# A state-space scan: the order of a round redone, one set of zero-weight products in place of two, and one copy from PSUM moved to VectorE

## What is computed

```python
def _ssm(h, in_w, xproj_w, dt_bias, A_log, Dskip, out_w):
    ...
    dt = jax.nn.softplus(proj[..., :D_INNER] + dt_bias)
    Bm = proj[..., D_INNER:D_INNER + D_STATE]
    Cm = proj[..., D_INNER + D_STATE:]
    A = -jnp.exp(A_log)
    def step(hst, ins):
        dt_t, B_t, C_t, x_t = ins
        dA = jnp.exp(dt_t[:, :, None] * A)
        hst = hst * dA + (dt_t * x_t)[:, :, None] * B_t[:, None, :]
        y_t = jnp.einsum('bds,bs->bd', hst, C_t)
        return (hst, y_t)
    _, ys = jax.lax.scan(step, h0, (tm(dt), tm(Bm), tm(Cm), tm(xs)))
    y = jnp.swapaxes(ys, 0, 1) + xs * Dskip
    return y * jax.nn.silu(z) @ out_w
```

## Time and profile before

| | us |
|---|---|
| median of 3 runs | 7119.47 (7112.84 to 7120.07) |
| the profiled execution | 7115.03 |
| its span, first to last instruction | 7113.3 |

### The profile page before, as it was taken

How to read it: one execution, slowest core, us unless ns; L and a number is a source line. 1 busy time by engine, 2 the same in 40 slices (tenths; PEclk the granted TensorE clock), 3 DMA queues, 4 the chain that set the end, 5 groups by cost and what they waited for, 6 DMA issues and landing times. The chain is left out here.

```text
span 7113.3 us, 205317 instructions
## 1 busy us (share of the span) xinstructions
PE 6393.6 (90%) x85792; PEld 3192.1 (45%) x85792; DVE 4188.9 (59%) x6974; ACT 4613.4 (65%) x9618; POOL 3331.1 (47%) x2816
## 2 busy tenths in 40 slices
PE   6888679999999999999999999979899999978988
PEld 3444434444444444444444444434355445444544
DVE  2555556666666666666666666655344445445554
ACT  3555478888888888888888888852244345345554
POOL 0011156666666666666666666640033223224432
PEclk8999879999999999999999999989999999989999
DMA  6555522222222222222222222235200000010000
GB/s 192 150 142 138 159 68 59 59 58 58 65 60 58 59 58 65 60 59 58 59 59 66 59 59 59 58 123 201 95 7 7 10 7 10 4 35 13 10 13 7
DMA packets 596363, 459.87 MB, mean 65 GB/s; under 512 B 449728, under 2 KB 504640, under 8 KB 577280
## 3 DMA queue, kind: packets, MB, share of 16 engines
q1 hardware_dynamic: 594408, 444.73, 21.5%
q10 hardware_dynamic: 1048, 2.16, 0.1%
HBM read 301.29 MB, written 145.49 MB: 63 GB/s over the span
## 5 line engine op out<-in xcount | busy, mean ns | idle before, releaser
L1472 POOL TENSOR_TENSOR s_dec<-s_hs,s_dec 128x512 f32<-128x512 f32 x2040 | 2561.5, 1281 | 1212.7 <-DVE s_hs L1512 791.9
L1393 ACT ACTIVATE s_dec<-s_pa 128x512 f32<-128x512 f32 x4096 | 2268.9, 618 | 403.8 <-PE s_pa L1246 403.6
L1501 DVE TENSOR_TENSOR s_pA<-s_pA,s_dec 128x512 f32<-128x512 f32 x2040 | 1393.0, 694 | 830.3 <-ACT s_hs L1399 563.9
L1512 DVE TENSOR_TENSOR s_hs<-s_pB,s_dec 128x512 f32<-128x512 f32 x2040 | 1330.9, 684 | 338.1 <-PE s_py L1283 236.8
L1283 PE MATMUL s_py<-s_hs,s_cz 128*32 128x256 f32 x16384 | 1392.4, 418 | 0.0
L1399 ACT COPY s_hs<-s_pA 128x512 f32<-128x512 f32 x2048 | 1210.3, 599 | 205.0 <-PE s_pA L1256 201.8
L1292 PE MATMUL s_py<-s_still 128*32 128x512 bf16 x15848 | 1243.2, 386 | 0.0
L1246 PE MATMUL s_pa<-s_dl,s_al 18*128 18x64 bf16 x32768 | 958.9, 192 | 79.7 <-DMA s_dl<-D 48.6
L1256 PE MATMUL s_pA<-az 18*128 18x256 bf16 x4096 | 778.7, 285 | 180.5 <-DVE s_pA L1501 176.5
L1256 PE MATMUL s_pB<-az 18*128 18x256 bf16 x4096 | 826.5, 283 | 3.5 <-DMA az<-U 3.5
L2067 POOL TENSOR_TENSOR t_prob<-t_prob,t_rinv 128x512 f32<-128x512 f32 x512 | 528.7, 1039 | 508.5 <-DVE t_rinv L2440 508.5
(11 more groups left out here) (260 smaller groups left out, 6395.2 us busy)
## 6 DMA issues: line engine op xcount, KB each, us to landing
s_dl<-D SPq DMA_DIRECT2D x512, 144.0 KB
az<-U SPq DMA_DIRECT2D x1024, 72.0 KB
az<-B SPq DMA_DIRECT2D x1024, 36.0 KB
D<-p_dp SPq DMA_DIRECT2D x64, 384.0 KB, 5.8
U<-p_up SPq DMA_DIRECT2D x60, 384.0 KB, 6.3
B<-p_bz SPq DMA_DIRECT2D x144, 128.0 KB, 2.5
SZ<-p_sz SPq DMA_DIRECT2D x16, 1024.0 KB, 4.0
SK<-p_skip SPq DMA_DIRECT2D x16, 1024.0 KB, 5.8
```

What stands on the lines that cost most here:

```text
L1393: act.activation(dec[w][:].rearrange("p k i t d -> p (k i t) d")[:, :, DS * q + d:DS * q + d + 8], pa[:, bank, :].rearrange("p (d c) -> p ...
L1472: pool.tensor_tensor(m, two(hs[k][:, (x + 1) % 2, :]), m, ALU.mult).then_inc(m_done, 1)
L1501: dve.tensor_tensor(state, state, of_chunk(k, x), ALU.mult).then_inc(mul, 1)
L1512: dve.tensor_tensor(out, two(pB[:, k - 2, :]), of_chunk(k, x), ALU.add).then_inc(added, 1)
```

## The change

- `keep_warm` makes one set instead of two, always onto `py`; the two calls onto `pB` in round 1 are gone.
- `adt` calls the hook before its third and fifth step instead of before its first and fourth.
- TensorE's order in a quiet round: A0; y of the round before last, half 1; a set; B3 of this round; w0 with A1 beside; y of the last round, half 0; a set; w1 with B2 of the next round beside. Rounds 0 and 8 begin with that y, the set, B3, w0, y half 0, a set and only then A0; then w1, A1, y half 1, B2. Rounds 1 and 9 have their own order.
- VectorE's order: multiply 0, addition 3 of the last round, multiply 1, addition 2. In rounds 0 and 8 the addition comes ahead of the wait for the decays. The addition of chunk 3 has thus moved from its own round into the next.
- `copied` becomes `copied0` and `copied1`. In rounds 7 and 15 VectorE makes the copy of chunk 1 (`copy_1`), ScalarE elsewhere.
- ScalarE's copy of chunk 0 also waits for `y_mm`, half 1 of the y of two rounds before.

```diff
                 def adt(p, w, banks, beside=None):
-                    if beside:
-                        beside(0)
                     wait(pe, taken, 2 * p - 1)
                     for i in range(8):
-                        if beside and i == 3:
-                            beside(1)
+                        if beside and i in (2, 4):
+                            beside(i // 2 - 1)
...
-                def keep_warm(onto):
-
-                    for _ in range(2):
+                def keep_warm():
+
+                    for _ in range(1):
                         for k in range(CH):
-                            pe.matmul(onto[QR * k:QR * (k + 1), :], still[:, W:W + QR], still[:, 0:W],
+                            pe.matmul(py[QR * k:QR * (k + 1), :], still[:, W:W + QR], still[:, 0:W],
...
+                        if x % TB == 0:
+                            if n:
+                                y(n - 2, (x - 2) % BODY, 1)
+                                keep_warm()
+                            to_b3()
+                            make(0, None)
+                            if n:
+                                y(n - 1, old, 0)
+                                keep_warm()
+                            to_a(n, x, 0, 0)
+                            to_a(n, x, 0, 1)
+                            make(1, None)
+                            to_a1(0)
+                            to_a1(1)
+                            if n:
+                                y(n - 1, old, 1)
                             to_b2(0)
                             to_b2(1)
...
+                        elif x % TB == 1:
+                            to_a(n, x, 0, 0)
+                            to_a(n, x, 0, 1)
+                            make(0, None)
+                            to_b3()
+                            if x == 9:
+                                keep_warm()
+                            to_a1(0)
+                            to_a1(1)
+                            if x == 1:
+                                make(1, None)
+                                wait(pe, ytok_done, G)
+                                wait(pe, c_filled, 2 * G + 1)
+                                y(n - 1, old, 0)
+                                keep_warm()
+                                to_b2(0)
+                                to_b2(1)
+                            else:
+                                wait(pe, c_filled, 2 * G + 2)
+                                y(n - 1, old, 0)
+                                keep_warm()
+                                make(1, to_b2)
+                        else:
+                            to_a(n, x, 0, 0)
+                            to_a(n, x, 0, 1)
+                            y(n - 2, (x - 2) % BODY, 1)
+                            keep_warm()
+                            to_b3()
+                            make(0, to_a1)
+                            y(n - 1, old, 0)
+                            keep_warm()
+                            make(1, to_b2 if ahead else None)
...
                 def copy_a(n, x, k):
+                    if k == 0:
+                        wait(act, y_mm, 2 * n - 2)
                     wait(act, bu_a, 2 * n + k + 1)
...
-                            copy_a(n, x, 1)
+                            if x % TB != TB - 1:
+                                copy_a(n, x, 1)
...
+                def copy_1(n, x):
+                    wait(dve, bu_a, 2 * n + 2)
+                    dve.tensor_copy(hs[1][:, x % 2, :], pA[:, 1, :]).then_inc(copied1, 1)
...
+                        if x % TB == 0 and n:
+                            plus(n - 1, 3)
                         dec_ready(dve, G, x, head)
-                        for k in range(2):
-                            times(n, x, k, start)
+                        times(n, x, 0, start)
+                        if x % TB:
+                            plus(n - 1, 3)
+                        times(n, x, 1, start)
                         if x == 1 and not head:
                             take_y(G)
-                        for k in range(2, CH):
-                            plus(n, made, x, k, start)
+                        plus(n, 2)
+                        if x % TB == TB - 1:
+                            copy_1(n, x)
```

More of the change, by code:

```diff
@@ L1113, in scan @@
         a_in = [sem(f"a_in{e}") for e in range(4)]
-        (c_in, y_out, zeroed, const, mul, bu_a, copied, bu_b, added, m_done, y_mm, filled, taken, c_filled,
+        (c_in, y_out, zeroed, const, mul, bu_a, copied0, copied1, bu_b, added, m_done, y_mm, filled, taken, c_filled,
          ytok_done, exp_ready) = (
-            sem(n) for n in ("c_in", "y_out", "zeroed", "const", "mul", "bu_a", "copied", "bu_b", "added", "m_done",
+            sem(n) for n in ("c_in", "y_out", "zeroed", "const", "mul", "bu_a", "copied0", "copied1", "bu_b", "added", "m_done",
                              "y_mm", "filled", "taken", "c_filled", "ytok_done", "exp_ready"))
@@ L1278, in y @@
                     if v == 0:
-                        wait(pe, copied, 2 * n + 2)
+                        wait(pe, copied0, n + 1)
+                        wait(pe, copied1, n + 1)
                         wait(pe, added, 2 * n + 2)
@@ L1317, in body, with to_a1 @@
                         more = not (last and x >= TB)
-                        late = x == 1
-                        before = (x - 1) % BODY
-                        has = not (head and x == 0)
                         ahead = not (last and x == BODY - 1)
-                        def to_a0(v):
-                            to_a(n, x, 0, v)
+                        old = (x - 1) % BODY
+                        def to_a1(v):
+                            to_a(n, x, 1, v)
                         def to_b2(v):
-                            if late and v == 0:
-                                wait(pe, added, 2 * n + 1)
-                                keep_warm(pB[:, 0, :])
@@ L1330, in to_b2 @@
                             to_b(n + 1, (x + 1) % BODY, G + (x + 1) // BODY, 2, v)
[L1332 to L1352, removed]
+                        def to_b3():
+                            if n:
+                                for v in range(2):
+                                    to_b(n, x, G, 3, v)
@@ new lines, in make @@
+                        def make(w, beside):
+                            if more:
+                                produce(G, x, w, head, turn, beside)
+                            elif beside:
+                                beside(0)
+                                beside(1)
+                        if x % TB == 0:
[12 more added lines that the diff above has]
+                            to_a1(1)
+                            if n:
+                                y(n - 1, old, 1)
@@ L1382, in _ @@
                 bodies(body)
+                y(BODY * ALL - 2, BODY - 2, 1)
                 y(BODY * ALL - 1, BODY - 1, 0)
@@ L1397, in copy_a @@
                 def copy_a(n, x, k):
+                    if k == 0:
+                        wait(act, y_mm, 2 * n - 2)
                     wait(act, bu_a, 2 * n + k + 1)
-                    act.copy(hs[k][:, x % 2, :], pA[:, k, :]).then_inc(copied, 1)
+                    act.copy(hs[k][:, x % 2, :], pA[:, k, :]).then_inc(copied1 if k else copied0, 1)
                 def take_pair(G, x, w, head):
@@ L1495, in times @@
                 def times(n, x, k, first):
-                    wait(dve, copied, 2 * n + k - 1)
+                    wait(dve, copied1 if k else copied0, n)
                     if first:
@@ L1501, in times, with plus @@
                         dve.tensor_tensor(state, state, of_chunk(k, x), ALU.mult).then_inc(mul, 1)
-                def plus(n, made, x, k, first):
+                def plus(n, k):
+                    G, x = n // BODY, n % BODY
+                    made = 2 * (n - G // BODIES)
                     wait(dve, bu_b, 2 * n + k - 1)
@@ L1507, in plus @@
                     out = two(hs[k][:, x % 2, :])
-                    if first:
+                    if n % (BODY * BODIES) == 0:
                         dve.tensor_copy(out, two(pB[:, k - 2, :])).then_inc(added, 1)
                     else:
-                        wait(dve, m_done, made + 2 * x + k - 3)
+                        wait(dve, m_done, made + k - 3)
                         dve.tensor_tensor(out, two(pB[:, k - 2, :]), of_chunk(k, x), ALU.add).then_inc(added, 1)
+                def copy_1(n, x):
+                    wait(dve, bu_a, 2 * n + 2)
+                    dve.tensor_copy(hs[1][:, x % 2, :], pA[:, 1, :]).then_inc(copied1, 1)
                 def take_y(G):
@@ L1523, in body @@
                         start = first and x == 0
+                        if x % TB == 0 and n:
+                            plus(n - 1, 3)
                         dec_ready(dve, G, x, head)
-                        for k in range(2):
-                            times(n, x, k, start)
+                        times(n, x, 0, start)
```

(9 more changed lines are left out.)

## The result

The changed kernel takes 6945.94 us, median of 4 runs (6929.75 to 7066.31), against 7117.27 us before; the ratio is 0.9754, with a 95% interval of 0.974 to 0.9767. Forecast were 6575 us and a range of 6460 to 6810: the direction was right, a third of the saving came.

A forecast was written before the change was run, and what follows sets the result against it. TensorE bounds quiet rounds by a hair (3.02 us), and seams cost 2.8 us each. A body of 50.5 us plus 0.7 for clock falls, times 64, gives a 3275 us scan, saving 538 from 7115: 6575 us, range 6460 to 6810.

The forecast's parts named there:

- The seam of round 8: Between blocks of 8 rounds: a seam costs 1.1 us instead of 2.8, round 8's exponentials no longer waiting for VectorE.
- The quiet round: In the scan: 2.92 us instead of 3.02, with ScalarE's 2.90 now longer than TensorE's 2.82.
- The body at full clock: Sixteen rounds of the scan: 16 x 2.92 + 1.1 + 1.27 + 1.4 = 50.5 us, before 59.6.
- The copy on VectorE: Rounds 7 and 15: 0.24 us won a seam, its 0.68 us costing nothing in 2.13 us of idle time.
- rival D: Seams: VectorE's copy locks out GpSimd on the path, up to 6660 us; chance 0.05.
- The loads: U and B loads in the scan: costed at nothing; 26 us if four runs a body came 0.1 us late each.
- The clock: In the scan: most bodies keep 2.4 GHz; one body in six falls, 4 us lost each, 0.7 a body.
- rival A: The clock falls in every body of the scan as before, 64 x 54.5 = 3488, 6790 us; chance 0.22.
- rival B: In the scan the clock does not come back up, rounds run at 4.9 us, at most 8560 us; chance 0.05.

The follow-up runs named there:

- gap_fill_half: The gap-filling kernel without the zero-weight set behind the first y of quiet rounds; 7043.93 us (6866.12 to 7124.9).
- gap-filling kernel: The changed kernel with seven more zero-weight sets a body where TensorE waits, in rounds 0, 1, 2, 8 and 9; 6601.78 us, again 6594.27 us.
- gap_fill_first: The changed kernel with only the four added zero-weight sets of rounds 0, 1 and 2; 6822.17 us, ratio 0.96 to before.
- two_sets: The changed kernel with two sets of zero-weight products a call instead of one; 7225.59 us, ratio 1.0156 to before.

## Why the prediction was wrong

1. The seam of round 8, right. The walk gives 8 x 2.92 + 1.1 = 24.5 us for the block of round 8, measured 24.32. Round 8 took 2.06 us as walked through, VectorE's idle time 1.24.
2. The quiet round, right: 2.94 against 2.92, with ScalarE unbroken; gap_fill_half, whose TensorE has a set less to do, has 2.94 too.
3. The body at full clock, right: 50.5 forecast, 50.91 and 50.64 in the two gap-filling kernels shown. The changed kernel itself has no body that is wholly at full clock.
4. The copy on VectorE, right in size: 0.24 us a seam walked, 0.18 measured at full clock and 0.26 in the whole time. But the prediction says that it runs beside GpSimd's product of chunk 3, and that is not so. GpSimd's last product before the seam shown ends at 2163.41 and the copy starts at 2163.45; in 127 of the 128 seams the two do not overlap. So this copy could not test rival D. VectorE's other PSUM copy, of `py`, could, as in the new order it does fall beside GpSimd's products:

```profile
2160.73 2.68 POOL L1494 TENSOR_TENSOR s_dec<-s_hs,s_dec 128x512 f32<-128x512 f32 x2 [1.36 <-DVE s_hs L1536]
...
2132.07 4.98 POOL L1494 TENSOR_TENSOR s_dec<-s_hs,s_dec 128x512 f32<-128x512 f32 x4 [2.59 <-ACT s_dec L1412]
2136.01 0.68 DVE L1546 COPY wa<-s_py 128x512 f32<-128x512 f32 x1
```

In 63 of 64 bodies it overlaps a product; both keep their durations, 0.68 and 1.28 us, and four products in a row take 4.98 us with the copy beside them, after 4.97 in the kernel before. D shows nowhere.

5. The loads: no term was needed. TensorE waits for U once in the scan, 1.7 us.
6. The clock, wrong, and it is nearly the whole miss. The step reads "most bodies should keep 2.4 GHz. ... I take one body in six", at 4 us lost a fall. At 64 x 50.91 = 3258 us the scan would have been 408 us shorter than its 3666, and 7115 - (3813 - 3258) = 6560 us. Instead some 1170 us went by at 1.2 GHz, each costing 0.35 us. The sum had 64 x 0.7 = 45 us for this. What was mis-sized is above all the number of falls: 90 and not 11. Their price was nearly right, 408 / 90 = 4.5 us and not 4, for a mean length of 12.6 us and not 10.2; the 20.48 us of the body shown is not typical. "One in six" had no row behind it. I compared the longest idle times with those of before and looked for the emptiest stretch of rounds 8 and 9 alone, and not at rounds 1 and 2, where all but one of the bodies fall, although rival A names the waits of round 1. And I set the thinned seam of round 8 beside one of before that had six zero-weight sets between its start and A1 of round 9, where the new order has two. The length depends on the sets: 7 to 10 us with two sets a call; with one, mostly 14 to 27 or just 3.4; up to 498 with one of its two calls gone.
7. Rival A named the right mechanism at too low a price: 4 us a body, where it was 408 / 64 = 6.4, as there was twice the time at 1.2 GHz in a body, 18 us after 8, part of it at the second seam. Part of rival B, held for 5 in 100, is there too: a quiet round at 1.2 GHz took 4.8 us, as it said, and in 27 of the 64 bodies more than half of the first block ran so. But the clock came back each time, after 48 us at most for stretches that begin in the scan, and the whole was faster, not slower.

Why the new order starts a second fall in rounds 9 and 10, even with two sets a call, no run separates: the places of A, B and y changed together.

The Trainium skill, TensorE: Matmul & The Clock Gate, Part 1, says that activity releases the throttle. Two kernels that differ in where seven sets stand (and in two waits), 6602 and 7003 us, agree with it as far as falling goes, and I had weighed it too lightly. For coming back it is not enough as it stands: gap_fill_half was busy for 415.93 of 418.00 us and stayed at 0.50.

## What to carry to other kernels

Work that only keeps TensorE's clock up has two uses here, and they sit in different places. Where the engine waits it prevents a fall, at almost no cost. In the busy rounds it prevents few falls (three begin in the scan with it, seven without), but without it they last longer: one set fewer in a quiet round cost 450 us by the medians. So thin such work by place and not by rate, and try each place by itself. After a change that shortens TensorE's work, price each round at both clock levels and ask separately what would start a fall and what TensorE is doing when the clock should come back. And judge an order by its rounds at full clock: with its idle places filled the changed kernel takes 0.93 of the time before, and without 0.975. How much of the 0.93 the new order alone is worth is not shown, since no run fills the idle places of the old order, which spent 540 us at 1.2 GHz itself.

## What the runs showed of the hardware

- At 1.2 GHz a TensorE that is busy without a printed gap (20.40 of 20.40 us in gap_fill_first, 415.93 of 418.00 in gap_fill_half) is not thereby given its clock back; with two zero-weight sets a call (before, two_sets) it came back after 7 to 10 us in nearly every body.
- The clock can fall without a long idle time. Just ahead of 85 of the changed kernel's 90 falls TensorE has no printed idle time over 0.35 us; before, the usual fall came behind one of 1.13.
- A float32 copy from PSUM on VectorE (0.68 us) and a float32 product of GpSimd (1.28 us) ran side by side 63 times without either taking longer.
- A body can be in step with the clock. In the second profile of the changed kernel bodies mostly follow each other in a cycle of three (a stretch of 20.5 us, one of 13.7 us, and two of 3.4 us). That may be why a shift of 0.2 us in a seam moved the total by some 100 us; no run tests it.
- The kernel whose clock hardly ever falls but stays down when it does has the widest spread, 6866 to 7125 us in four executions; the gap-filling kernel has 6589 to 6620 in eight.
